# Edge attention: one transposing pass over gathered score columns instead of four small products, and another bank for the drops

## The reference

```python
hs = (x @ Ws + bs).reshape(N, H, HD)          # H = 8 heads of HD = 96
hd = (x @ Wd + bd).reshape(N, H, HD)
hs_e = hs[src]
e = jax.nn.leaky_relu(hs_e + hd[dst], SLOPE)
logits = jnp.einsum('ehd,hd->eh', e, attn)
m = jax.ops.segment_max(logits, dst, num_segments=N)
ex = jnp.exp(logits - m[dst])
s = jax.ops.segment_sum(ex, dst, num_segments=N)
alpha = ex / s[dst]
out = jax.ops.segment_sum(alpha[..., None] * hs_e, dst, num_segments=N)
```

## Time and profile before

| | |
|---|---|
| device time, median of 3 runs | 2290.42 us (2289.82 to 2291.83) |
| span of the profiled execution | 2290.0 us |
| TensorE busy, share of the span | 2152.8 us, 94% |
| VectorE busy | 1648.9 us, 72% |
| ScalarE busy | 1124.0 us, 49% |
| GpSimd busy | 883.9 us, 39% |
| macro-tiles of the attention | 2 x 91 |

### The profile page before, as it was taken

The page is one execution under the profiler, slowest core; times in us unless marked ns, Lnnn a source line. Parts: engine busy times, 40 slices in busy tenths (PEclk is TensorE's granted clock), DMA queues, the critical chain, the costliest instruction groups (busy, mean ns, idle before and its releaser), DMA issues. The chain is left out here.

```text
span 2290.0 us, 88815 instructions
## 1 busy us (share of the span) xinstructions
PE 2152.8 (94%) x32341; PEld 1719.5 (75%) x32341; DVE 1648.9 (72%) x4252; ACT 1124.0 (49%) x2759; POOL 883.9 (39%) x847
## 2 busy tenths in 40 slices
PE   5999999998999999999998899899999999999788
PEld 3665555555889888998887556688888888888676
DVE  5224997343888888888888764488888888888884
ACT  1101210023666666666664424466666666666584
POOL 0000001111556666566562311365556555556121
PEclk9999999999999999999998999999999999999889
DMA  5000124343778787788774124488787777777411
GB/s 189 1 0 17 70 97 101 105 121 92 241 246 249 246 244 246 246 256 249 249 236 143 69 85 130 139 248 246 247 250 238 245 238 242 243 233 244 167 54 47
DMA packets 139458, 401.25 MB, mean 175 GB/s; under 512 B 21704, under 2 KB 76267, under 8 KB 139123
## 3 DMA queue, kind: packets, MB, share of 16 engines
q0 software_dynamic: 59584, 298.64, 42.6%
q1 hardware_dynamic: 76525, 90.41, 12.5%
q10 hardware_dynamic: 3044, 7.45, 1.0%
HBM read 368.18 MB, written 16.78 MB: 168 GB/s over the span
## 5 line engine op out<-in xcount | busy, mean ns | idle before, releaser
L496 ACT ACTIVATE at_relu<-at_turned,ah_attn_size 128x512 f32<-128x512 f32 x1092 | 719.1, 694 | 471.7 <-PE at_turned L555 470.3
L477 POOL DMA_INDIRECT at_rows<-table,ah_index x360 | 398.5, 1107 | 281.5 <-DVE ah_index L679 163.9
L477 POOL DMA_INDIRECT ah_room<-table,ah_index x352 | 392.3, 1115 | 267.3 <-DVE ah_index L679 176.5
L553 PE MATMUL at_turned<-ah_place,dst_rows 96*128 96x128 bf16 x2208 | 402.7, 223 | 26.9 <-issue 16.9
L555 PE MATMUL at_turned<-ident,ah_room 128*128 128x128 f32 x2208 | 419.1, 280 | 2.4 <-issue 2.4
L555 PE MATMUL at_turned<-ident,at_rows 128*128 128x128 f32 x2160 | 405.3, 278 | 4.3 <-issue 4.3
L553 PE MATMUL at_turned<-at_place,dst_rows 96*128 96x128 bf16 x2160 | 389.6, 222 | 2.0 <-issue 1.5
L675 DVE SCALAR_TENSOR_TENSOR sums<-sums,at_factor,at_total 128x97 f32 x1456 | 343.7, 309 | 3.2 <-issue 0.8
L555 PEld LDWEIGHTS at_turned<-ident,ah_room 128*128 128x128 f32 x2208 | 318.4, 144 | 30.9 <-issue 6.6
L665 DVE TENSOR_TENSOR at_spread<-at_lined,at_weight 128x1024 f32<-128x1024 f32 x182 | 223.0, 1225 | 164.1 <-ACT at_weight L506 115.6
L555 PEld LDWEIGHTS at_turned<-ident,at_rows 128*128 128x128 f32 x2160 | 308.3, 143 | 27.0 <-issue 5.1
(11 more groups left out here) (311 smaller groups left out, 3150.4 us busy)
## 6 DMA issues: line engine op xcount, KB each, us to landing
at_flags<-run_flags SPq DMA_DIRECT2D x182, 64.0 KB
dst_rows<-pr_parts SPq DMA_DIRECT2D x76, 144.0 KB, 2.6
ah_place<-local_rows SPq DMA_DIRECT2D x92, 96.0 KB
at_place<-local_rows SPq DMA_DIRECT2D x90, 96.0 KB
table<-ah_room SPq DMA_DIRECT2D x20, 400.0 KB, 2.4
ah_room<-table,ah_index POOLq DMA_INDIRECT x368
at_rows<-table,ah_index POOLq DMA_INDIRECT x360
mx_w<-in_L_mix_W_qkv SPq DMA_DIRECT2D x2, 2304.0 KB, 18.6
```

The lines of the kernel that those rows point to most:

```text
L477: pool.indirect_dma_start(rows[b][:, j, :], None, table, bass.IndirectOffsetOnAxis(index[b][:, j:j + 1], 0)).then_inc(gathered[b], 16)
L496: act.activation(relu[c][:], turned[chunk(b, c)][:], ACT.Relu, scale=attn_size[:, c:c + 1]).then_inc(bent, 1)
L553: pe.matmul(into, dst_rows[:, bass.ds(at[j], 1), c * P:(c + 1) * P].rearrange("p o d -> p (o d)"), place[b][:, j * P:(j + 1) * P], start=T ...
```

## The change

The four products L563 go. In their place VectorE copies the 4 x 8 linear parts of every edge into a tile `linear` of four blocks of 32 columns (`line_linear`), whose other columns were set to zero once. TensorE turns that tile with one transposing pass of 128 x 128 into the bank `heads` (`turn_linear`), which opens the sum that L567 and L571 then add to. The pass is issued one slot earlier than the products were: after `sum_drops` of the macro-tile before and ahead of chunk 5 of its own. `sum_drops` now writes to columns 128 to 135 of the bank `back`, with a wait for the weights that are read from that bank, and `factors` reads them there. The waits at the head of `sum_heads` go with the products; `turn_linear` waits for the copy and for the shift of the macro-tile before. VectorE's copy stands between `build_place` and `spread_out`, and waits for the gathered rows and for chunk 5 of the macro-tile before. At the start, the one-time zeroing is that of `linear` instead of `heads`.

```diff
+        linear = sb("at_linear", [P, G, S])
...
                 def factors(m, b):
                     act.wait_ge(turned_back, 2 * m + 2)
                     for j in range(G):
-                        act.activation(factor[b % 2][:, j, :], heads[:, P + j * HH:P + (j + 1) * HH], ACT.Exp,
+                        act.activation(factor[b % 2][:, j, :], back[:, P + j * HH:P + (j + 1) * HH], ACT.Exp,
...
+                def turn_linear(m):
+                    pe.wait_ge(linear_ready, m + 1)
+                    pe.wait_ge(scanned, m * SCANS + (SCANS - 1))
+                    pe.matmul(heads[:, 0:P], linear[:].rearrange("p j r -> p (j r)"), ident[:], is_transpose=True, start=True, stop=False)
+
                 def sum_heads(m, b):
-                    pe.wait_ge(scanned, m * SCANS + SCANS)
-                    pe.wait_ge(weights_ready, m * EXPS + EXPS)
-                    for j in range(G):
-                        pe.matmul(head_row(j), rows[b][:, j, D + 1::QUAD], ident[:], start=True, stop=False)
                     for c in ALONE:
...
                 def sum_drops(m):
                     pe.wait_ge(dropped, m + 1)
-                    pe.matmul(heads[:, P:P + G * HH], head_rows[:], drop[:], start=True, stop=True).then_inc(turned_back, 1)
+                    pe.wait_ge(weights_ready, m * EXPS + (EXPS + 1))
+                    pe.matmul(back[:, P:P + G * HH], head_rows[:], drop[:], start=True, stop=True).then_inc(turned_back, 1)
...
                     if turn:
+                        turn_linear(turn[0])
                         turn_chunk(*turn, at, 5)
...
                 pe.wait_ge(merge_ready, 1)
+                pe.wait_ge(weights_ready, NM * EXPS + EXPS)
...
+                def line_linear(m, b, round, fresh):
+                    dve.wait_ge(gathered[b], landed(layer, b, round + 1))
+                    if not fresh:
+                        dve.wait_ge(turned_done, m * KC)
+                    dve.tensor_copy(linear[:, :, 0:H], rows[b][:, :, D + 1::QUAD]).then_inc(linear_ready, 1)
...
-                def slot(head, message, after=None, fresh=False, more=False):
+                def slot(head, message, turn=None, after=None, fresh=False, more=False):
...
                     if after:
                         build_place(*after)
+                    if turn:
+                        line_linear(*turn, head is None)
                     if head:
                         spread_out(head[0], head[1])
...
-                dve.memset(heads[:, 0:P], 0.0).then_inc(cleared, 1)
+                dve.memset(linear[:], 0.0).then_inc(cleared, 1)
...
-                slot(None, None, macro(0, 2))
-                slot(macro(0, 0), None, None, fresh=True)
+                slot(None, None, macro(0, 0), macro(0, 2))
+                slot(macro(0, 0), None, macro(0, 1), fresh=True)
                 with dve.Fori(0, LOOPS) as i:
                     for b in range(UNROLL):
-                        slot(macro(i, b + 1), macro(i, b), macro(i, b + 3), more=True)
-                slot(macro(LOOPS, 1), macro(LOOPS, 0))
+                        slot(macro(i, b + 1), macro(i, b), macro(i, b + 2), macro(i, b + 3), more=True)
+                slot(macro(LOOPS, 1), macro(LOOPS, 0), macro(LOOPS, 2))
```

More of the change, by code:

```diff
@@ L375 @@
               "turned_back", "weights_ready", "lined_ready", "spread_ready", "totalled", "added", "firsts", "merge_ready", "merged",
-              "merge_seen", "joined")
+              "merge_seen", "joined", "linear_ready")
 def attend_signals(nc):
@@ L427, in attend @@
         (cleared, index_ready, index_seen, place_ready, turned_done, bent, heads_done, scanned, raised, dropped, turned_back, weights_ready,
-         lined_ready, spread_ready, totalled, added, firsts, merge_ready, merged, merge_seen, joined) = sems[0:len(AT_SIGNALS)]
+         lined_ready, spread_ready, totalled, added, firsts, merge_ready, merged, merge_seen, joined, linear_ready) = sems[0:len(AT_SIGNALS)]
         local_loaded, flags_loaded, gathered = (
```

## The result

The changed kernel takes 2281.78 us (median of 6 runs, 2279.26 to 2285.10), the kernel before beside it 2291.12. The ratio is 0.9943 with a 95% interval of 0.9922 to 0.9964: faster by 8 to 18 us. The forecast was 2270, its range 2261 to 2283. So the sign and the range hold, but the gain is smaller than the 20 us forecast (9 us between the medians, 13 by the ratio), and as the rows show it came from another place. Executions in a slower state (2458 us with the index late, 7501 with the index last, 2813 and 12200 of the kernel before) are left out of all times here.

A forecast was written before the change was run, and what follows sets the result against it. TensorE's own stream, 7.12 us a lap, was taken as the bound. 2290.0 - 20.0 (products and pass) - 2.5 (stops) + 0.9 (layer start) + 1.0 (second loop) = 2269.4, rounded to 2270 us; range 2261 to 2283.

The forecast's parts named there:

- The four products go: TensorE's stream loses the L563 products and their free waits: 0.22 us less per macro-tile.
- The pass comes: TensorE's stream gains one transposing pass behind `sum_drops`: 0.11 us per macro-tile, at most 0.19; uncovered load 2283, chance 0.05.
- The second loop: Two-macro-tile loop through ScalarE's weights, VectorE's spread and shift, TensorE's L577: 7.005 to 7.06 us, +1 us; rival 2278, chance 0.08.
- The waits of the pass: On TensorE, waits for VectorE's copy and shift, with 1.2 us of cover for the copy: no steady-state cost.
- VectorE's copy: Copy of 0.2 to 0.35 us in VectorE's idle time before the spread: no cost while below 0.58.
- the drops' bank: Drops written to and read from the other bank, same product and shape: no cost.
- The start of a layer: TensorE's chunk 5 waits about 0.5 us for VectorE's first copy: +0.9 us over both layers.
- The stops: TensorE's 57 us of waits for instructions, falling 4.5% with the instruction count: -2.5 us.
- The clock: Rival: less arithmetic in TensorE's array brings the half level, 1.2 GHz; up to 2396 us, chance 0.01.
- the cited rule: Trainium skill's rule that TensorE's transposing passes don't count as activity holding the full clock rate; no size in the sum.
- VectorE as the bound: Rival: the copy with its waits, between `place` and spread, makes VectorE set the lap; 2310 us at 0.8, chance 0.03.
- the stops swallow a shorter lap: Rival: TensorE reaches the end of its fetched instructions sooner and waits longer; 2288 to 2292 us, chance 0.04.

The follow-up runs named there:

- index late: Changed kernel with VectorE's copy of the index list moved behind the first maximum: 2245.9 us, 0.9802 of the kernel before.
- index last: Changed kernel with VectorE's copy of the index list moved behind the copy of the linear parts: 2263.1 us, 0.9866 of the kernel before.
- split adds: Changed kernel with VectorE's adds of tiles 2 and 3 and its index list copy moved behind the first maximum: 2244.1 us, 0.9789 of the kernel before.
- drops alone: Kernel before with only the drops' product, its wait and the factors' reads moved to the bank `back`: 2295.3 us, 1.0016 of the kernel before.
- the loop: Changed kernel with TensorE's 22 x 4 slots as a real loop of 4 slots instead of one long stream: 2259.6 us, 0.9859 of the kernel before.

## Why the prediction was right or wrong

**The four products go: -0.22 per lap.** Right: L569 now follows the messages where L563 did.

**The pass comes: +0.11.** Mis-sized, and within its bounds of 0.11 to 0.19: it costs 0.14 behind the drops, whose narrow products don't cover its load (0.22 us long there), and 0.11 ahead of them. TensorE's stream is 7.06, seen as the lap of the split adds; the term is -0.07 x 182 = -13 us, not -20.

**The second loop: +1 us.** This is the step that failed, though the total came out within the range. I followed the loop over ScalarE's weights and VectorE's spread and put it at 7.005 to 7.06. The loop that binds is another, of one lap: messages, adds, scans, shift, `turn_back`, chunks, messages. From the numbers above it was 1.26 + 3.14 + 0.15 + 2.43 = 6.98 before (2.43 is 1008.29 - 1005.86; 3.14 is 1005.62 less the add's start a lap before, 1009.60 - 7.12), 0.14 below the lap; I took VectorE's string of work from the spread to the shift as unbroken, which it was only as long as the totals were there before VectorE asked for them. The change takes its 0.22 outside that loop and puts 0.14 (and about 0.03 more behind an L579 that had to wait: 2.61 - 2.43 is 0.18) inside. The whole lap term, -20 + 1 us, came out as +5. The sign that the prediction named for its second loop, L577 waiting for the shift in many laps, did appear: the step from the product ahead to L579 is 0.18 us in the median, where it was 0.11. It doesn't tell the two loops apart; the index copy behind the first maximum does, since the lap fell by all of the 0.07 and not by half.

**The waits of the pass, VectorE's copy, the drops' bank: nothing.** Right, by the copy done twice and, as far as the noise lets it be told, the drops alone. The copy takes 0.26 us where it stands (median), more than the 0.2 taken and the 0.19 estimated, and well inside the 0.58 of room. The idle time before the spread is 0.33, between the 0.25 and 0.4 given.

**The start of a layer: +0.9.** About right. The profile shows TensorE waiting for the first copy in both layers, here in layer 0:

```profile
572.95 0.33 PE L563 MATMUL at_heads<-ident,at_linear 128*128 128x128 f32 x1 [0.36 <-DVE at_linear L687]
```

In layer 1 the wait is 0.25. With the pass itself, 0.15 each, that is 0.9 us; all that is not laps grew by 1.1.

**The stops: -2.5.** That they are TensorE waiting for its code is shown by the loop and by the packets that land ahead of each. The size is wrong: -17 in the profiled executions. They don't go by the count of instructions alone. In these executions +5 by the laps, -17 by the stops and +1 outside them make the -11 between the spans. That the prediction's range held is luck, and owed to this term: with the stops as they were, the changed kernel would have been about 6 us slower than the kernel before, outside the range.

**The rivals.** The clock stayed at 1.00, so the harm that the cited rule would have brought didn't come; with 26 transposing passes among the 148 products of a lap, the run doesn't test the rule by itself. VectorE as the bound didn't happen. The rival that the stops swallow a shorter lap is nearest to what the experiments show, from the other side: with the changed instructions and early gathers, laps of 7.120, 7.154, 7.158 and 7.287 have stops of 47, 38, 33 and 17 us, so the mean lap is 7.38, 7.37, 7.34 and 7.38 whatever the lap. I read this as the delivery of instructions, not the lap, setting the time in this state, so that a shorter lap alone would have brought little. The pass ahead of the drops fits it (lap 0.034 shorter, time the same), but it is argued, not shown: each of these edits also moves the gathers against the stream. With the instructions of the kernel before it was 7.43 (both the kernel before and the drops alone). Whether the 0.06 between them comes from the 4.5% fewer instructions or from the gathers' moment, which moved a little too, no run isolates.

**What stays open.** Why the moment of the gathers matters to the instruction queue. On the kernel before, three positions of the index copy give fewer stops the later the gathers start; on the changed kernel the best start is about 0.8 us behind L579, and later ones are worse. The instruction packets ahead of a stop start late rather than take long; what holds up their start isn't shown by these traces.

## What to carry to other kernels

When work moves on a busy engine, ask not only how much shorter its stream gets, but in which loops through other engines the removed and the added piece stand: here 0.22 us left a stretch that ran in parallel to VectorE and 0.14 came into the one that closes the loop. Add up each loop, with the hand-overs, also those that an engine's idle time doesn't show yet, and give the margin of each. In the kernel before, by the same 1.26 the totals were ready at 1008.29 + 1.26 = 1009.55, only 0.05 us before VectorE's add took them up: so small a margin is a bound in waiting.

For an engine whose code is one long stream, look at how often the laps are longer than the shortest one before anything else. Here most of 55 us, several times what the change brought, hung on the place of one 0.17 us copy that starts the gathers; moving it gave 40 us in the kernel before and 36 in the changed one. The fastest version tried, the changed kernel with split adds, takes 2244.1 us, 0.9789 of the kernel before; the index copy alone is not to be told from it.

## What the runs showed of the hardware that I had not expected

- TensorE's instructions come by DMA in packets of 16 KB (4.34 MB in 265 packets of all code of the changed kernel), and the gathers' timing alone moved the stops from 55 to 32 to 15 us on one and the same lap. After a stop TensorE resumes about 1.4 us behind the landing of the last packet (medians of 1.35 to 1.45 us by kernel).
- A body of four laps, about 1200 of TensorE's products and loads (4 x 2 x 148), stayed in place in a loop: 52 packets instead of 265, at 0.38 us of idle time per round for the jump, with laps 0.40 to 0.55 us longer.
- The same transposing pass of 128 x 128 in float32 cost 0.11 us behind a full transposing pass, 0.14 behind products of 8 columns, and 0.37 between products that write strips of 32 partitions.
- The hand-over from VectorE's shift to TensorE's L579 is 0.12 us to the start of the load in the written-out stream and 0.05 in the loop (medians of layer 0); why, no run isolates.
